# One core, fused linear attention and mixture of experts: the first tile's chain ahead of the weight copies, and the Silu table with shared halves inside the last routed pair

## The reference

```python
x = x + attn(_layernorm(x), Wq, Wv, q_norm_w, v_norm_w)
x = x + ffn(_layernorm(x), Wg, W1, W2, W3, Ws1, Ws2, Ws3)

# attn: 16 heads of width 16, no softmax, a running state
Q = rms_norm_multihead(X @ Wq.T); V = rms_norm_multihead(X @ Wv.T); K = X
W = cumsum(einsum('blhd,blhe->blhde', K, V), axis=1)
out = einsum('blhd,blhde->blhe', Q, W)

# ffn: 4 experts of 32 per token, and the shared one
scores = softmax(xf @ Wg); weights, indices = top_k(scores, 4)
for e in range(32):  # its tokens, weighted
    y[tok] += (silu(xg @ W1[e]) * (xg @ W3[e]) @ W2[e]) * w
z = silu(xf @ Ws1) * (xf @ Ws3) @ Ws2
return y + z
```

## Time and profile before

| | value |
|---|---|
| median of 3 runs | 558.83 us (557.15 to 560.71) |
| the profiled execution's own time | 559.33 us |
| its span in the profile | 557.4 us |
| PE busy | 527.4 us (95%) |
| DVE busy | 382.2 us (69%) |
| ACT busy | 376.5 us (68%) |
| POOL busy | 331.8 us (60%) |

### The profile page before, as it was taken

One profiled execution on the slowest core, in us unless ns is written; L12 is line 12 of the kernel. 1 busy time (PEld: TensorE's weight loads), 2 busy tenths in 40 slices (PEclk: granted clock), 3 DMA queues, 4 the chain that ended last, 5 costly groups with the idle time before them and its releaser, 6 DMA issues.

```text
span 557.4 us, 18176 instructions
## 1 busy us (share of the span) xinstructions
PE 527.4 (95%) x5177; PEld 383.1 (69%) x5177; DVE 382.2 (69%) x1354; ACT 376.5 (68%) x1258; POOL 331.8 (60%) x367
## 2 busy tenths in 40 slices
PE   6798999999999999699999999999999999997996
PEld 2355666666666665357998988999999995544554
DVE  7698999999999996664444444444444446744786
ACT  2687899988989985402766766777677776653452
POOL 6010377776777777771665555666666564446992
PEclk8999999999999999899999999999999999998999
DMA  8998355556456554954676776766666554428999
GB/s 259 316 292 264 125 217 211 187 215 227 186 198 246 188 192 152 366 194 127 195 219 201 221 225 199 214 193 194 194 193 198 180 187 145 143 79 342 408 409 347
DMA packets 65088, 123.29 MB, mean 221 GB/s; under 512 B 9824, under 2 KB 44000, under 8 KB 64992
## 3 DMA queue, kind: packets, MB, share of 16 engines
q1 hardware_dynamic: 47824, 78.07, 44.1%
q0 software_dynamic: 13056, 39.86, 19.2%
q10 hardware_dynamic: 4112, 4.19, 2.3%
HBM read 58.49 MB, written 63.60 MB: 219 GB/s over the span
## 4 chain that ended last, share of the span: by engine, by line
PE 79%; DMA 5%; DVE 4%; issue 4%; ACT 3%; POOL 2%; SPq 1%; ACTq 1%; DVEq 0%; POOLq 0%
PE pS L967 18%; PE pQV L828 10%; PE pS L985 9%; PE pS L741 8%; PE pS L795 5%; PE pO L888 5%; DMA xg<-xs 3%; PE pO L869 3%; PE pT L946 3%; PE pQV L946 2%; PE pQV L757 2%; PE pO L757 2%; PE pT L774 2%; PE pO L803 2%; PE pT L817 1%
## 5 line engine op out<-in xcount | busy, mean ns | idle before, releaser
L495 POOL DMA_INDIRECT ys<-gsh,dst x144 | 138.1, 959 | 108.3 <-ACT gsh L663 86.6
L467 POOL DMA_INDIRECT xs<-xg,posi x128 | 123.8, 967 | 52.1 <-issue 31.4
L967 PE MATMUL pS<-after_a,x2T_all 128*128 128x128 f32 x1024 | 135.5, 276 | 0.0
L967 PEld LDWEIGHTS pS<-after_a,x2T_all 128*128 128x128 f32 x1024 | 124.5, 192 | 0.0
L1375 DVE TENSOR_TENSOR after_a<-after_a,pS 128x128 f32<-128x128 f32 x144 | 41.5, 288 | 79.9 <-ACT after_a L651 76.1
L1346 DVE COPY x2T_all<-w 128x512 f32 x144 | 63.9, 444 | 32.9 <-issue 32.5
L985 PE MATMUL pS<-w,after_a 128*128 x256 | 76.7, 381 | 0.0
L1089 DVE TENSOR_TENSOR w<-pS,tri 128x512 f32<-128x512 f32 x96 | 65.1, 679 | 1.0 <-PE pS L795 1.0
L828 PE MATMUL pQV<-w 128*128 128x512 f32 x128 | 63.7, 621 | 0.5 <-ACT w L533 0.5
L663 ACT ACTIVATE gsh<-pS,xg 128x256 f32<-128x256 f32 x128 | 60.6, 474 | 0.4 <-issue 0.4
L662 ACT CAST dst<-xg 128x1 int32 x128 | 24.5, 191 | 45.3 <-PE pS L985 43.3
(11 more groups left out here) (221 smaller groups left out, 1019.8 us busy)
## 6 DMA issues: line engine op xcount, KB each, us to landing
xg<-xs SPq DMA_DIRECT2D x128, 160.0 KB, 2.8
ys<-gsh SPq DMA_DIRECT2D x32, 512.0 KB
w<-ys SPq DMA_DIRECT2D x32, 512.0 KB, 15.3
w<-in_L_ffn_W ACTq DMA_DIRECT2D x1, 4096.0 KB, 18.6
out<-xall SPq DMA_DIRECT2D x14, 256.0 KB, 7.2
xs<-padrow SPq DMA_DIRECT2D x32, 80.0 KB
xg<-xs SPq DMA_DIRECT2D x32, 80.0 KB, 2.2
ys<-gsh,dst POOLq DMA_INDIRECT x144
```

Of the source, the lines that this page charges most:

```text
L467: pool.indirect_dma_start(out=xs, out_offset=bass.IndirectOffsetOnAxis(ap=posi[:, a.r8, k:k + 1], axis=0), in_=xr[:, a.r8, :], in_offset=N ...
L495: pool.indirect_dma_start(out=ys, out_offset=bass.IndirectOffsetOnAxis(ap=dst[:, j % 8:j % 8 + 1], axis=0), in_=y[:, j % 8, :], in_offset= ...
L967: last = pe.matmul(pS[a.b][:, n * P:(n + 1) * P], w13_staged(a.t)[:, (2 * k + n) * F:(2 * k + n + 1) * F], xgT[:, a.b, k, :], start=(k == ...
```

## The change

At the start, tile 0 gets a DMA of its own (`x_head`, 128 KB), ahead of the weights, and tiles 1 to 3 follow the weights. DVE computes tile 0's mean and variance in the middle of its constants, POOL its root ahead of four masks. PE waits for one copied weight half, not two, before it transposes tile 0, then multiplies zeros once (256 columns) and waits for the second. Statistics run 5 tiles ahead instead of 6. Three constants that the attention state needs move behind tile 0's sum of squares.

At the end of attention, ACT loads the Silu table after the last pair's logits were copied out for transposing (L585), and does `shared_silu(0)` there; after the copy of the last logits (L581) it loads the table of exponent and logarithm again, and after the loop Silu a second time. PE does two halves behind the last logits instead of after the row count, and one more, (2, 0, 1), ahead of the count. DVE does both gates of group 0 inside the last step of the loop. The kept half of group 3 is done wholly ahead of the expert loop: on PE both halves, on ACT its Silu, on DVE its product.

```diff
-            sp.dma_start(xall[:, 0:4, :], x_tiles[:, 0:4, :]).then_inc(S["x_first"], 16)
+            sp.dma_start(xall[:, 0:1, :], x_tiles[:, 0:1, :]).then_inc(S["x_head"], 16)
             sp.dma_start(wq_in, Wq.rearrange("(k p) c -> p k c", p=P)).then_inc(S["w_in"], 16)
             sp.dma_start(wv_in, Wv.rearrange("(k p) c -> p k c", p=P)).then_inc(S["w_in"], 16)
+            sp.dma_start(xall[:, 1:4, :], x_tiles[:, 1:4, :]).then_inc(S["x_first"], 16)
...
@@ gpsimd @@
             chain(pool.memset(head_mask[:], 1.0))
+            rstd1(0)
...
             assert c[0] == HEAD_CONSTS
-            rstd1(0)
             rstd1(1)
...
@@ scalar, step @@
                     act.copy(lg[:, a.pb].rearrange("p h e -> p (h e)"), pT0[:, P:P + 2 * E]).then_inc(S["lg_done"], 1)
+                    if a.t == NT - 1:
+                        act.preload_act_table_set("natural_log_exp_and_others")
...
                     act.copy(lgT[:], pT0[:, 0:P]).then_inc(S["lgT_done"], 1)
+                    if a.t == NT - 1:
+                        act.preload_act_table(ACT.Silu)
+                        shared_silu(0)
...
                     if a.t == 0:
-                        act.wait_ge(S["consts_dve"], DVE_CONSTS)
+                        act.wait_ge(S["consts_dve"], QM_CONSTS)
...
             act.preload_act_table(ACT.Silu)
...
-            for g in range(NPRE):
+            for g in range(1, NPRE):
                 shared_silu(g)
+            half_silu(NPRE, 0)
...
                 if (a := tile_of(0)) is not None:
-                    if a.t == 1:
-                        half_silu(NPRE, 0)
...
@@ tensor @@
-            pe.wait_ge(S["wt_done"], KC)
+            pe.wait_ge(S["wt_done"], 1)
...
                 if (a := tile_of(0)) is not None:
+                    if a.t == 0:
+                        keep_busy(1, 256)
+                        pe.wait_ge(S["wt_done"], KC)
...
                     pe.matmul(pT0[:, P:P + 2 * E], lgT[:], pick, start=True, stop=True).then_inc(S["logits_ps"], 1)
+                    if a.t == NT - 1:
+                        pe.wait_ge(S["x2T_done"], NT)
+                        pe.wait_ge(S["silu_done"], 1)
+                        shared_half(1, 1, 1)
+                        pe.wait_ge(S["silu_done"], 2)
+                        shared_half(2, 0, 0)
...
+            pe.wait_ge(S["gsh_done"], 1)
+            shared_half(2, 0, 1)
             pe.wait_ge(S["mcum_done"], NT)
             pe.wait_ge(S["rk_done"], NP2)
             pe.matmul(pT0[:, 0:E], ones16[:], mcum[:, 0, 0, :], start=True, stop=True).then_inc(S["cnt_ps"], 1)
-            pe.wait_ge(S["x2T_done"], NT)
-            pe.wait_ge(S["silu_done"], 1)
-            shared_half(1, 1, 1)
-            pe.wait_ge(S["silu_done"], 2)
-            shared_half(2, 0, 0)
-            pe.wait_ge(S["gsh_done"], 1)
-            shared_half(2, 0, 1)
...
                     last.then_inc(S["xT_ps"], 1)
-                    if a.t == 0:
-                        shared_half(NPRE, 0, 1)
...
             shared_half(NPRE, 0, 0)
+            shared_half(NPRE, 0, 1)
             pipelined(NJ, 4, expert_step)
...
@@ vector @@
             chain(dve.tensor_copy(eidx[:], eidx_i[:]))
+            dve.wait_ge(S["x_head"], 16)
+            stats1(0)
+            mean1(0)
...
             chain(dve.tensor_copy(dst_f[:], dst_i[:]))
+            bias1(0)
...
                         dve.tensor_tensor(mcum[:, a.pb, 1, :], mcum[:, a.pb, 0, :], mask[:, a.pb, 0, :], ALU.add
                                       ).then_inc(S["mcum_done"], 1)
+                    if a.t == NT - 1:
+                        dve.wait_ge(S["ys_zeroed"], 16 * ZC)
+                        shared_gate(0)
...
-                if (n := tile_of(-6)) is not None:
+                if (n := tile_of(-5)) is not None:
...
                     dve.tensor_reduce(ss[:, a.r4, 0:2 * H], sq.rearrange("p (h e) -> p h e", e=d), AX_X, ALU.add
                                       ).then_inc(S["ss_done"], 1)
+                    if a.t == 0:
+                        for g in range(KC):
+                            chain(dve.tensor_scalar(head_mask[:, g, :], head_mask[:, g, :], wqc[:, g:g + 1], None, ALU.mult))
+                        chain(dve.tensor_copy(padrow[:, DST:DST + E], pdst_i[:]))
...
-            dve.wait_ge(S["ys_zeroed"], 16 * ZC)
-            half_gate(0, 0)
-            half_gate(0, 1)
...
             shared_add(2)
+            dve.wait_ge(S["silu_done"], FC * NPRE + 1)
+            dve.tensor_tensor(sg[:, 0, :], sg[:, 0, :], h_bank(NPRE, 0, 1)[:], ALU.mult).then_inc(S["kept"], 1)
             dve.wait_ge(S["w2_in"], 16)
```

More of the change, by code:

```diff
@@ L517, in normalise, with half_silu, shared_silu @@
                 act.activation(xn[:, t % 3, :], xall[:, t, :], ACT.Identity, bias=bias, scale=scale).then_inc(S["xn_done"], 1)
+            def half_silu(g, m):
+                wait(act, S["h_ps"], FC * g + m + 1)
+                wait(act, S["gsh_done"], FC * (g - 1) + m + 1)
+                act.activation(sg[:, m, :], h_bank(g, m, 0)[:], ACT.Silu).then_inc(S["silu_done"], 1)
+            def shared_silu(g):
+                for m in range(FC):
+                    half_silu(g, m)
             normalise(0)
@@ L619, in _ @@
             act.preload_act_table(ACT.Silu)
-            def half_silu(g, m):
-                wait(act, S["h_ps"], FC * g + m + 1)
-                wait(act, S["gsh_done"], FC * (g - 1) + m + 1)
-                act.activation(sg[:, m, :], h_bank(g, m, 0)[:], ACT.Silu).then_inc(S["silu_done"], 1)
-            def shared_silu(g):
-                for m in range(FC):
-                    half_silu(g, m)
-            for g in range(NPRE):
+            for g in range(1, NPRE):
                 shared_silu(g)
+            half_silu(NPRE, 0)
             number = [[act.alloc_register(f"act_expert{h}_{n}") for n in range(4)] for h in range(2)]
@@ L1053, in _ @@
             dve.wait_ge(S["x_first"], 16)
[L1054 to L1062 removed]
+            for t in range(1, 4):
+                stats1(t)
+                mean1(t)
             dve.wait_ge(S["x_second"], 16)
@@ L1066, in _ @@
             bias1(1)
-            for t in range(5, lead_a):
-                stats1(t)
-                mean1(t)
             dve.wait_ge(S["zeros_dve"], 1)
```

41 lines of the change are left out of this document (13 added, 28 removed).

## The result

The changed kernel took 561.83 us (median of 16 runs, 559.17 to 566.45) against 559.39 (557.1 to 561.45, 16 runs) for the kernel before on the same chip: ratio 1.0045, interval 1.0025 to 1.0065. So it is slower by 2.5 to 3.2 us, where 0.15 less was forecast. The median itself lies above the forecast's upper edge of 561.4; put on the 558.83 of the runs before, the first ratio gives 561.3. Either is within 1% of the forecast. The profiled execution took 566.19 us (span 564.4), 4.4 above the median, so its stretches are read and not its end.

The account below looks back on a forecast made before the run. PE held 79% of the chain, so the change was read where PE is not fed. Start -0.45 plus middle +0.6 gave 0.15 gained: 559.2 us profiled, 558.7 us as median against 558.83; range 555.8 to 561.4.

Parts of the forecast that it names:

- The start's chain: Tile 0's path: q and v at 8.4, sum of squares at 12.9, q transposes at 15.9, leaving 0.95 us gained.
- The clock at the start: PE's clock falls in a 2.4 us gap before 15.9, slowing tile 1's q and v and transposes by 1.4 us.
- L828 should run at full clock and end near 10.35, not 13.63: Tile 0's q and v: PE without a gap from 6.24 on, 3.3 us gained, most of it then given back.
- the forecast for the start, 0.45 lost: Start of the kernel: 0.95 gained less 1.4 for the clock's fall at tile 1, a loss of 0.45 us.
- Between attention and experts: Last logits to block 0: ranks and count later, DVE's table chain shorter, kept half 0.6 lost; together 0.6 us gained.
- PE, at full clock, has finished its halves and group 0 at 241.4: Before the table's rows: PE is early and DVE becomes the bound, at most 2.2 us gained.
- The sum of DVE's chain: DVE's table chain from the count: 14.7 us less two gates (1.2) and a 2.63 wait gives 10.9, ending at 245.3.
- PE's idle 3.9: Before the table's rows: PE, finished at 241.4, waits 3.9 us for DVE, and its clock should fall.
- the low clock behind the rows: After PE's wait: the rows take 1.9 us instead of 0.96, and first results of group 1 twice as long.
- 0.6 was to be gained: Attention's end to block 0: gain of 0.6 us with a brief low clock, 0.9 lost with a long one.
- slower: the low clock lasts long: Both places: start loses 1.45 us, middle 0.9, together 2.35, giving 561.1 us; chance 0.18.
- The hidden gains: Experts' blocks start when POOL's scatters allow, needing late loads: 558.8 us, or 2 to 3 either way; chance 0.07.

Follow-up runs that it names:

- the start alone: Kernel before with only the start of the change: 559.49 us, ratio 0.9999; on the slow chip 701.53 us, 1.0028.
- the run that filled the wait: Changed kernel with two idle copies of half (2, 1, 1) on PE between the second and third result of z(0): 560.66 us, ratio 1.0011.
- the mended kernels: Changed kernel, or its second half alone, with DVE's first two adds early and further repairs, in several versions: ratios from 0.9977 to 1.0009.
- the end alone: Kernel before with only the change between attention and experts: ratio 1.0031; on the slow chip 693.61 us, 0.9916.

## Why the prediction was wrong

**The start's chain** had the right links and a missing wait. Tile 0's statistics began at 3.49 (forecast 3.5 to 3.8). L836 took 2 us at full clock, but at 9.28 and not at 8.4: the weight transposes took 1.91 and not 1.09, since the clock rose late. That cost nothing further, because DVE was the later one: in the kernel with the kept half put back on the slow chip, the transposes took 1.04 and q and v began at 8.30, and the sum of squares still stood at 13.70. The forecast let tiles 1 to 3 be there when DVE came to them; their load, moved behind 512 KB of weights, was 1.16 late in the first profile. Hence the sum of squares at 13.66, not 12.9, and the q transposes at 16.36, not 15.9. Where the wait was nil, they stood at 15.21.

**The clock at the start** was forecast to fall at tile 1, at 1.4. It does so in some executions and not in others. The larger slip is on the other side of the sum: "L828 should run at full clock and end near 10.35, not 13.63" was set against the 3.27 of the earlier trace rows, as if these belonged to the old start. Three of seven profiles have them at 1.98. That the forecast for the start, 0.45 lost, lies near what the means show at tile 3 (0.5, or 0.95 on ordinary chips) is luck: the terms differ, single profiles spread over 4 us, and the start alone measured no loss (0.9999, 0.9972 to 1.0027).

**Between attention and experts** the parts up to the count were right to a few tenths: Silu table at 227.0 (226.7), ranks at 232.6 (232.2), DVE's first use of the count at 234.7 (234.4), halves at full clock. The table loads began 0.01 to 0.02 us behind the end of the instruction before them, and the next instruction 0.01 to 0.02 behind theirs, at all three places. "ScalarE: Activation LUTs", section "What ACT_TABLE_LOAD costs", of the Trainium skill gives 1.38 us of drain on top for each switch to another set; the trace does not agree.

The step that failed is "PE, at full clock, has finished its halves and group 0 at 241.4". It counted PE's work and not what the work waits for: the third result of z(0) needs a bank that DVE empties at 242.93. The sum of DVE's chain took away the 2.63 of waiting for the second product and left the adds where they stood in the order; so DVE's 10.9 and PE's idle 3.9 were both near in size (DVE's chain measured 12.8, of which 2.25 was waiting for PE; PE's wait 4.45), and in the wrong order. With the adds moved, the stretch from count to rows measures 10.97 to 11.12, except 12.2 with the count moved too. As it was, 14.4 to 15.1: PE's idle time lay ahead of two results and a half of a 512-column product that the rows wait for, and ran them at low clock (2.07 and 1.91 a result, where 1.03 is full), and DVE's last adds waited for those in turn (1.23 in the fence above). The forecast put the low clock behind the rows. By the two middles 2.0 is lost, where 0.6 was to be gained: a miss of 2.6 us, as large as that of the whole.

The runs part this loss: the kept half costs 0.76 (forecast 0.6), the low clock 2.5 (one profile, of the run that filled the wait), and 2.5 + 0.76 - 2.0 leaves some 1.3 that the early halves win even with the wait for the bank. That last figure is what is left over and was not measured by itself.

**The rival** "slower: the low clock lasts long" (561.1) came nearest to the time, and its long low clock is there (6.9 us at 0.51); it gave 0.9 lost for the middle and 1.45 for the start, and it too had the low clock behind the rows. The range was widened by the spread of the runs at its lower side only (556.1 to 555.8); the upper edge, 561.4, stayed that of the worst case. The hidden gains, with little behind them in the forecast, are real in the mended kernels: 0.3 to 1.0 us of waiting for the first loads.

**The rest of the kernel** has no part in it that the profiles show. The first profile of the change lay 2.2 us behind at block 0, 4.4 at the last block and 7.0 at the end, which looked like a loss in the experts. Over eight profiles each, from block 0's first product to that of the last block it is 199.5 us with the straight order and 199.5 with the old, each between 197.7 and 201.3. From there to the end it is 97.7 and 97.3 on average, and 99.7 in that first profile. So the middle's 2.0 is the part of the measured 2.5 to 3.2 that is shown: the end alone lost 1.7 in time. What the start adds stays open, between nothing by its time and 0.5 to 1.0 by the profiles.

## What to carry to other kernels

When an engine is made early, look at every wait in its code that had never been the late one: a pair of PSUM banks used by turns ties a producer to the place of its consumer in another engine's order, and that place was chosen while the producer was late. Move the consumer together with the producer. And a low clock seen in one profile is a property of that execution until several profiles show it; do not book its removal as a gain.

## What the runs showed of the hardware

The granted clock behind a wait of PE between 2.2 and 2.5 us is not decided by the code: the same instructions kept it in some executions and lost it in others. Behind 2.2 us at the start it fell in three of nine profiles at once and in a fourth one tile later, behind 2.4 us ahead of the table's rows in four of seven; behind 4.4 us it fell in all four on ordinary chips, and in the old start behind waits of 1.68, 1.96 and 2.02. Behind 1.1 us there it fell in none of three, though behind 1.24 it did on the slow chip (L832 of tile 0 in 2.90). The granted clock of the changed kernel's second profile at tile 1, and of the end alone at tile 0 (columns as the earlier trace rows):

```profile
16.13:23.05 6.92, 5.75 (x25) 2.60 (x25) 2.66 (x9) 3.64 (x11) 0.00 (x0) 0.58 1.09 331
```

```profile
10.25:12.20 1.95, 1.95 (x6) 0.95 (x7) 1.74 (x9) 0.45 (x1) 1.62 (x7) 1.00 1.07 375
```

The second surprise is the chip that ran every kernel in about 700 us, with engines standing still for up to 12 us. On it the end alone measured 0.9916, on another 1.0031: the same edit with the sign turned, probably because early work fills stops that other chips do not have. What makes that chip stop was not found.
